# Decoder layer with attention, cross-attention and a gated FFN: other places in the rounds for score blocks, maxima, projections, splits and the gate step

## What is computed

```python
def _L0_attn_ref(x, Wq, Wk, Wv, Wo, gamma, beta):
    q = x @ Wq.T
    k = x @ Wk.T * scale
    v = x @ Wv.T
    ...
    qk = jnp.where(causal, qk, -jnp.inf)
    attn = jax.nn.softmax(qk, axis=-1)
    ...
    return ln @ Wo.T
...
x = x + _L0_attn_ref(_layernorm(x, axis=-1), ...)
x = x + _L0_xattn_ref(ctx_1024, ctx_1024, _layernorm(x, axis=-1), ...)
x = x + _L0_ffn_ref(_layernorm(x, axis=-1), ...)
...
    gates = entmax_bisect(logits)
    gates = jnp.where(gates > THRESH, gates, 0.0)
    h = jax.nn.relu(jnp.einsum('td,edf->etf', xt, W1) + b1[:, None, :])
    y = jnp.einsum('etf,efd->etd', h, W2) + b2[:, None, :]
    out = jnp.einsum('etd,te->td', y, gates)
```

## Time and profile before

| what | value |
|---|---|
| median of 3 runs | 665.8 us (664.77 to 667.24) |
| profiled execution | 664.33 us |
| its span, first to last instruction | 662.6 us |
| busy: PE, DVE, ACT, POOL | 93%, 70%, 62%, 55% |
| granted clock of PE, mean | 0.991 |
| length of rounds 0 to 6, from H 0 to the next H 0 | 72.85, 73.45, 73.59, 73.59, 73.60, 73.56, 66.63 us |
| round 7 and the end | 55.2 us |

### The profile page before, as it was taken

How to read it: one execution, slowest core, us unless ns; L and a number is a source line. 1 busy time by engine, 2 the same in 40 slices (tenths; PEclk the granted TensorE clock), 3 DMA queues, 4 the chain that set the end, 5 groups by cost and what they waited for, 6 DMA issues and landing times.

```text
span 662.6 us, 15729 instructions
## 1 busy us (share of the span) xinstructions
PE 618.6 (93%) x5263; PEld 459.8 (69%) x5263; DVE 464.3 (70%) x996; ACT 408.0 (62%) x780; POOL 363.9 (55%) x599
## 2 busy tenths in 40 slices
PE   5488879999999999999999999999999999998997
PEld 3355557777677767777678767777677767776775
DVE  4495984679747986689747986599557984656544
ACT  4239476755777566755766557755776567665543
POOL 8625565445663737444763746544753756464363
PEclk9889999999999999999999999999999999999999
DMA  6705100530027000630036000720045000700230
GB/s 187 230 17 169 45 4 18 127 117 4 19 45 208 10 8 14 151 107 2 18 67 191 0 20 0 162 95 2 18 98 159 2 2 6 159 2 1 55 88 16
DMA packets 39195, 43.76 MB, mean 66 GB/s; under 512 B 2922, under 2 KB 23670, under 8 KB 39158
## 3 DMA queue, kind: packets, MB, share of 16 engines
...
...
## 4 chain that ended last, share of the span: by engine, by line
PE 77%; DVE 8%; ACT 6%; POOL 3%; issue 2%; DMA 2%; SPq 2%; ACTq 0%; DVEq 0%; POOLq 0%
PE h_ps L1038 10%; PE y_ps L1038 9%; PE h_ps L1040 8%; PE h_ps L1039 8%; PE y_ps L1040 8%; PE y_ps L1039 8%; DVE negmax L1657 5%; PE sbuf_m L1149 5%; PE sbuf_s L1132 3%; PE sbuf_s L1104 2%; ACT prob L1462 2%; PE sbuf_s L1149 2%; PE sbuf_s L1053 1%; PE sbuf_s L1066 1%; PE sbuf_m L1038 1%
## 5 line engine op out<-in xcount | busy, mean ns | idle before, releaser
L1773 DVE SCALAR_TENSOR_TENSOR h_lo<-h_ps,h_hi 128x512 fp32r<-128x512 f32 x256 | 172.2, 682 | 120.3 <-ACT h_hi L1481 119.4
L1481 ACT ACTIVATE h_hi<-h_ps 128x512 fp32r<-128x512 f32 x256 | 152.1, 601 | 129.7 <-PE h_ps L1040 127.7
L1038 PE MATMUL h_ps<-fT_lo,w_hi 128*128 128x512 f32 x256 | 111.6, 436 | 4.1 <-DVE fT_lo L1626 2.7
L902 POOL TENSOR_SCALAR_AFFINE_SELECT prob<-prob 128x512 f32<-128x512 f32 x128 | 79.8, 642 | 60.7 <-ACT prob L1462 57.2
L1462 ACT ACTIVATE prob<-sbuf_s 128x768 f32<-128x768 f32 x124 | 95.2, 813 | 25.7 <-PE sbuf_s L1132 25.7
L1038 PE MATMUL y_ps<-h_lo,w_hi 128*128 128x512 f32 x255 | 106.9, 419 | 1.5 <-ACT y_sb L1490 1.5
L1657 DVE TENSOR_REDUCE negmax<-sbuf_s 128x4 f32<-128x1024 f32 (+1 forms) x91 | 106.9, 1212 | 0.1
L1039 PE MATMUL h_ps<-fT_hi,w_lo 128*128 128x512 f32 x256 | 101.2, 395 | 0.0
L1040 PE MATMUL h_ps<-fT_hi,w_hi 128*128 128x512 f32 x256 | 101.1, 395 | 0.0
L1040 PE MATMUL y_ps<-h_hi,w_hi 128*128 128x512 f32 x255 | 100.8, 395 | 0.0
L1039 PE MATMUL y_ps<-h_hi,w_lo 128*128 128x512 f32 x255 | 100.7, 395 | 0.0
...
## 6 DMA issues: line engine op xcount, KB each, us to landing
...
```

The source lines that it names most:

```text
L902: pool.affine_select(out=v, in_=v, compare_op=ALU.is_ge, fill=0.0, base=0, pattern=[[0, 2], [0, 2], [1, P]], channel_multiplier=-1).then_i ...
L1038: pe.matmul(out_ap, w_hi, m_lo, start=start, stop=False)
L1481: act.activation(h_hi[:, c % HB, :], h_ps[:, c % 2, :], ACT.Relu).then_inc(hhi_made, 1)
L1773: dve.scalar_tensor_tensor(out=h_lo[:, c % HB, :], in0=h_ps[:, c % 2, :], scalar=0.0, in1=h_hi[:, c % HB, :], op0=ALU.max, op1=ALU.subtrac ...
```

## The change

Numbers in the tables Z_STEPS, A_STEPS and X_STEPS are others; no function changes, no step is added or taken away, and the first phase and the last store are as before. All rounds are affected. A few of the lines of the diff, those that the text below speaks of:

```diff
-    Step("MAX", 6, "s", pe=26.02, dve=26.01),
-    Step("MAX", 7, "t", pe=26.03, dve=26.02),
-    Step("MT", 0, "m", pe=27.01, dve=26.03, sp=1.5),
+    Step("MAX", 6, "s", pe=26.02, dve=25.5134),
+    Step("MAX", 7, "t", pe=26.5255, dve=26.019),
+    Step("MT", 0, "m", pe=27.017, dve=26.5403, sp=1.5),
...
-    Step("MT", 1, "s", pe=32.51, dve=31.01, sp=1.75),
-    Step("SC", 2, "s", pe=33.51, act=33.51, pool=7.25),
-    Step("SC", 3, "t", pe=33.52, act=33.52, pool=7.5),
+    Step("MT", 1, "t", pe=32.5233, dve=31.5177, sp=1.75),
+    Step("SC", 2, "s", pe=33.5049, act=35.001, pool=7.25),
+    Step("SC", 3, "t", pe=40.5171, act=38.0238, pool=7.5),
...
-    Step("NA", 2, "-", act=31.01),
-    Step("T3", 0, "m", pe=32.52, act=31.02, dve=31.02),
+    Step("NA", 2, "-", act=30.503),
+    Step("T3", 0, "m", pe=32.51, act=32.5218, dve=33.5204),
...
-    Step("TH", 0, "-", pool=0),
+    Step("TH", 0, "-", pool=0.5),
...
-    Step("GV", 0, "-", dve=7.01),
+    Step("GV", 0, "-", dve=6.02),
...
-    Step("GT", 0, "m", pe=9.51, act=9.52, sp=0.25),
+    Step("GT", 0, "m", pe=10.0113, act=9.52, sp=0.25),
```

More of the change, by code:

```diff
@@ L78 @@
 Z_STEPS = [
[L79 to L86, removed]
+    Step("SZ", 0, "-", dve=8.5162, pool=2.75),
+    Step("NZ", 0, "-", act=12.5242),
+    Step("T1", 0, "t", pe=14.0063, act=14.0174, dve=14.0075),
@@ L87 @@
+    Step("Q", 0, "m", pe=16.0132, act=15.5254, dve=15.0077),
+    Step("K", 0, "s", pe=16.5178, act=16.0037, dve=16.0094, sp=1.25),
+    Step("V", 0, "t", pe=16.5269, dve=16.0165),
+    Step("MAX", 0, "s", pe=21.51, dve=21.0096),
+    Step("MAX", 1, "t", pe=22.5153, dve=21.5186),
     Step("MAX", 2, "s", pe=23.51, dve=23.01),
-    Step("MAX", 3, "t", pe=23.52, dve=23.02),
+    Step("MAX", 3, "t", pe=24.5197, dve=23.0227),
     Step("MAX", 4, "s", pe=25.01, dve=24.02),
-    Step("MAX", 5, "t", pe=25.02, dve=24.03),
@@ L101 @@
-    Step("SC", 2, "s", pe=33.51, act=33.51, pool=7.25),
-    Step("SC", 3, "t", pe=33.52, act=33.52, pool=7.5),
+    Step("MAX", 5, "t", pe=26.0193, dve=24.5335),
+    Step("MAX", 6, "s", pe=26.02, dve=25.5134),
+    Step("MAX", 7, "t", pe=26.5255, dve=26.019),
+    Step("MT", 0, "m", pe=27.017, dve=26.5403, sp=1.5),
+    Step("MAX", 8, "s", pe=28.5083, dve=28.0125),
+    Step("MAX", 9, "t", pe=29.0146, dve=28.0245),
+    Step("SC", 0, "s", pe=29.51, act=29.51, pool=6.5),
+    Step("SC", 1, "t", pe=30.0203, act=29.52, pool=6.75),
@@ L103 @@
+    Step("MAX", 10, "s", pe=30.51, dve=30.0102),
+    Step("MAX", 11, "t", pe=30.518, dve=30.5183),
+    Step("MT", 1, "t", pe=32.5233, dve=31.5177, sp=1.75),
+    Step("SC", 2, "s", pe=33.5049, act=35.001, pool=7.25),
+    Step("SC", 3, "t", pe=40.5171, act=38.0238, pool=7.5),
     Step("XL", 0, "-", sp=0),
@@ L106 @@
 A_STEPS = [
[L107 to L116, removed]
@@ L117 @@
-    Step("SC", 12, "s", pe=10.51, act=9.53, pool=2.75),
-    Step("SC", 13, "t", pe=10.52, act=9.54, pool=3.25),
+    Step("PV", 0, "m", pe=1.5203, act=4.5089),
+    Step("SC", 4, "s", pe=1.5379, act=1.5058, pool=0),
+    Step("SC", 5, "t", pe=2.0331, act=1.5198, pool=0.25),
+    Step("SC", 6, "s", pe=3.5086, act=3.5153, pool=0.75),
+    Step("SC", 7, "t", pe=4.0216, act=3.5266, pool=1),
+    Step("SC", 8, "s", pe=5.0086, act=5.0196, pool=1.5),
+    Step("SC", 9, "t", pe=6.0084, act=5.0246, pool=2),
@@ L119 @@
+    Step("PV", 1, "m", pe=6.0108, act=6.5048),
+    Step("SC", 10, "s", pe=6.0198, act=6.5219, pool=2.25),
+    Step("SC", 11, "t", pe=7.0198, act=7.5058, pool=2.5),
+    Step("SC", 12, "s", pe=10.51, act=9.53, pool=3),
+    Step("SC", 13, "t", pe=10.5146, act=9.5385, pool=3.25),
     Step("PV", 2, "m", pe=10.52, act=9.55),
     Step("SC", 14, "s", pe=11.02, act=10.01, pool=3.5),
-    Step("SC", 15, "t", pe=11.03, act=10.02, pool=3.75, sp=0.75),
-    Step("BT", 0, "s", pe=12.01, dve=10.02),
-    Step("BT", 1, "m", pe=12.02, dve=12.01),
+    Step("SC", 15, "t", pe=11.5314, act=10.0163, pool=3.75, sp=0.75),
@@ L124 @@
+    Step("BT", 0, "s", pe=12.01, dve=10.5201),
+    Step("BT", 1, "m", pe=12.02, dve=10.5206),
     Step("PV", 3, "t", pe=12.03, act=12.01),
-    Step("SA", 0, "-", dve=12.04, pool=4),
+    Step("SA", 0, "-", dve=12.039, pool=4),
     Step("BT", 2, "t", pe=12.51, dve=12.02),
[L127 to L137, removed]
-    Step("NA", 2, "-", act=31.01),
-    Step("T3", 0, "m", pe=32.52, act=31.02, dve=31.02),
+    Step("BT", 3, "m", pe=12.52, dve=12.03),
+    Step("NA", 0, "-", act=15.5127),
+    Step("TA", 0, "m", pe=18.0101, act=18.0075, dve=18.0084),
@@ new lines @@
+    Step("WO", 0, "s", pe=19.5132, dve=19.5116),
+    Step("SA", 1, "-", dve=20.5127, pool=5.25),
+    Step("NA", 1, "-", act=23.5086),
+    Step("T2", 0, "m", pe=24.5099, act=24.5121, dve=24.0109),
+    Step("XS", 0, "m", pe=26.0056, act=26.0103, dve=25.5068),
+    Step("PT", 0, "s", pe=27.0159, act=26.0109, dve=26.5217),
+    Step("SA", 2, "-", dve=28.0373, pool=6.25),
+    Step("XO", 0, "m", pe=28.5245, dve=28.0259),
+    Step("NA", 2, "-", act=30.503),
+    Step("T3", 0, "m", pe=32.51, act=32.5218, dve=33.5204),
@@ L143 @@
 X_STEPS = [
-    Step("TH", 0, "-", pool=0),
-    Step("LG", 0, "s", pe=1.01, dve=1.01),
+    Step("TH", 0, "-", pool=0.5),
+    Step("LG", 0, "s", pe=1.01, dve=1.5076),
     Step("TH", 1, "-", pool=1.25),
-    Step("TH", 2, "-", pool=1.5),
+    Step("TH", 2, "-", pool=1.75),
     Step("YM", 0, "-", pool=4.25),
     Step("YM", 1, "-", pool=4.5),
-    Step("YM", 2, "-", pool=5),
-    Step("YM", 3, "-", pool=5.25),
+    Step("YM", 2, "-", pool=4.75),
+    Step("YM", 3, "-", pool=5),
     Step("YM", 4, "-", pool=5.5),
@@ L154 @@
     Step("CP", 0, "-", pool=6),
-    Step("YM", 6, "-", pool=6.5),
-    Step("GV", 0, "-", dve=7.01),
+    Step("YM", 6, "-", pool=7),
+    Step("GV", 0, "-", dve=6.02),
     Step("YM", 7, "-", pool=7.75),
-    Step("GT", 0, "m", pe=9.51, act=9.52, sp=0.25),
+    Step("GT", 0, "m", pe=10.0113, act=9.52, sp=0.25),
 ]
```

## The result

The changed kernel takes 677.26 us (median of four runs, 675.96 to 678.37) against 665.79 for the kernel before, run beside it: a ratio of 1.017, 95% interval 1.014 to 1.02. It is slower by 1.7%, as forecast, and the time is 1.3 us over the 676.0 predicted. The profiled execution took 676.36 us (span 674.6) against 664.33 (662.6).

What follows compares the result with a forecast made beforehand. PE's issue order was taken to bound the kernel (PE busy 93% of the span). Losses of 9.0 + 0.7 + 1.6 = 11.3 us on 664.33 gave 675.6, or 677.1 from the median; forecast 676.0, range 668.5 to 680.0.

Steps and rivals of the forecast that it cites:

- The signs that I named: Trace signs: 1.2 us gap before H9, DVE idle over 1 us, mass at H0 + 15.8, excess 0.3 later, rounds 75.1.
- Place 1: GV ahead of l7 on DVE waits for POOL's gate chain, delaying H9: 1.04 + 0.25 us in rounds 0 to 6.
- The 0.25 for excess: After H0, SC4's mask on POOL runs beside L1722 on DVE and stretches it, so TH0 starts 0.25 us later.
- the 0.12 that I priced for it: By the shared-port rule POOL's first mask waits for L1718, TH0 some 0.12 us later; kept out of the sum.
- Place 2: Round border: MAX6 early makes drop_a, NA2, h31, l31 late, so next H0 is 0.26 us later, in six rounds.
- the terms of a tenth that it left out: Two opposite terms of about a tenth: later exps of SC2 and SC3, and H10 no longer behind GV.
- Most other moves pass under cover: Other reordered steps have inputs ready before their engine arrives and readers half a slot later or more, so cost nothing.
- block switches stay as many: On PE each small block keeps a neighbour of the same kind, so switches between block kinds do not change.
- The small loss: Rival: GV misses POOL's masks and takes 1.0 us, stall 0.3 before H9; about 669.5 us; chance 0.14.
- No difference: Rival: the mass comes a whole microsecond earlier, l7 is in time and the border stays; 665.8 us; chance 0.13.
- Faster: Rival: PE's three stops behind Y27 close, l31 ending by about 391.4; 1.1 us a round, about 659 us; chance 0.09.
- The larger loss: Rival: POOL resumes late behind the round's border, 0.7 us more a round; 681 us; chance 0.04.

Runs made afterwards that it cites:

- e2: Kernel before with only GV moved ahead of l7 on DVE; 675.06 us, ratio 1.0119, rounds 1 to 5 mean 74.62 us.
- e5: Changed kernel with GV, the seven border steps and GT put back; 666.95 us, ratio 0.9979 to the kernel before, rounds 73.29 us.
- e3: Changed kernel with the seven border steps put back, GV still ahead of l7; 676.45 us, ratio 1.0118 to the kernel before, rounds 74.34 us.
- e4: Changed kernel with GV and the seven border steps put back; 668.45 us, ratio 1.0015 to the kernel before, rounds 73.79 us.
- e1: Changed kernel with only GV put back behind l7 on DVE; 671.94 us, ratio 1.0057 to the kernel before, rounds 74.21 us.
- e8: Changed kernel with POOL's SZ moved right behind TH2, so no mask runs beside GV; 679.29 us in a single run, rounds 75.08 us.

## Why the prediction was right, and where not

**Direction and mechanism: right.** GV ahead of l7 is the loss: 1.06 us a round alone (e2), and 1.05 in the whole change as well (e5 to e3, 73.29 to 74.34, together with GT). The signs that I named are in the trace, some of them at another size: the gap before H9 put down to h_lo (a bracket of 0.76, for about 1.2), DVE idle for 1.99 between l6 and GV, the mass at H0 + 15.81, excess later (by 0.52, for 0.3; it is 0.32 in e3 and e4, and the rest is the 0.20 of l0 and l1), a wait that goes from before MT1 to before T3 and Y31, and rounds of 74.76, for about 75.1.

**Place 1, 1.29 a round: too high by a quarter of a microsecond.** Measured are 1.05. The 0.25 for excess have a real cause: L1722 beside SC4's mask took 0.74 instead of 0.43, in the changed kernel and in e4 alike, and TH0 starts 0.32 later in e4 than before. Here is e4:

```profile
328.06 0.43 DVE L1718 TENSOR_TENSOR over<-below 128x256 f32<-128x256 f32 x1
328.52 0.74 DVE L1722 SCALAR_TENSOR_TENSOR over<-over 128x256 f32<-128x256 f32 x1
```

```profile
328.34 1.42 POOL L902 TENSOR_SCALAR_AFFINE_SELECT prob<-prob 128x512 f32<-128x512 f32 x2 [0.36 <-ACT prob L1462]
329.91 0.30 POOL L934 TENSOR_SCALAR moments<-excess 128x32 f32<-128x32 f32 x1 [0.15 <-DVE excess L1725]
```

With that, the working has H9 at H0 + 18.56, and it stands at 18.32. The 0.24 are three pieces: the mass came at 15.81 and not 15.62 + 0.25 = 15.87; GV follows it by 0.08 and not by 0.2; and l7 starts 1.69 behind GV's start and not 1.74. The 18.32 hold the 0.13 of the late SC4, which belong to the border; in e3, which is without them, the mass comes at 15.71 and H9 at 18.22, so against that the working is 0.34 too late, and half of it is the mass. Its sums also slip by 0.02 to 0.03 on the way (326.68 is carried on as 326.66; 330.14 + 2.95 + 0.81 is 333.90 and not 333.87), which changes nothing.

The rule of the Trainium skill, "SBUF — State Buffer", section "Who interferes with whom", that a two-input DVE instruction and a GpSimd instruction reading SBUF exclude each other, would have made POOL's first mask wait for L1718. In e4 the first mask starts at 328.34, while L1718 runs until 328.49, and the 0.12 that I priced for it are not there: TH0 is 0.32 late, the 0.34 of the sum without the rule. That DVE is held up is seen; that POOL is, at most in the second mask of the pair (1.42 for two, where four took 2.41).

**Place 2, 0.26 a round: too low.** 0.42 (after to e3, e4 to e1). I had the chain (MAX6 late, drop_a late, NA2, h31, l31, MT1, T3), and it makes 0.27 in e1 as priced. But I counted only what shows at the border; the other 0.15 are the late SC4 in the next round, which the working put among the terms of a tenth that it left out (the later exps of SC2 and SC3). One line of the working does not add up as it stands: 392.47 and 0.08 + 0.76 + 0.69 are 394.00, and 393.84 comes out with the 0.08 taken off. The trace has it the second way: MT1 is drawn as starting 0.08 ahead of l31's end, and from l31's end to T3's on DVE it is 1.36, for 1.37.

**"Most other moves pass under cover": wrong, they gain 0.27 a round.** I wrote that PE stands still only behind Y27. It also waited for l8 at H10, 0.13 a round, where the timeline names no gap. And I wrote that block switches stay as many; between Q and WO the moves give back 0.14, for a reason that stays open. GT's move behind H10 is not in the working at all (its term of a tenth at H10 was GV's); it costs 0.4 to 0.5 by itself, though it seems to cost nothing beside GV's new place.

**The sum.** Rounds 0 and 6 lose more at H9 than the five between them (it stands 1.16 later in round 0 and 1.67 in round 6, and GV is 2.3 long in both); round 7 loses the 0.7 that I worked out (0.69). Place 1: 1.16 + 5 × 1.05 + 1.67 + 0.69 = 8.8, for 9.7. Border: 6 × 0.42 = 2.5, for 1.6. The others: about 6 × −0.27 = −1.6, for 0. Together 9.7, for 11.3, and the rounds grew by 9.8; how round 0 divides among the three is taken from the other rounds, not measured. That the profiled time was still 676.36, over the 675.6 of the sum, is the 2.2 us ahead of round 0. So three terms were off by about 0.9, 0.9 and 1.6 us, these 2.2 were not foreseen, and that the total came within 1.3 us is luck; the direction and the largest term are not.

**The rivals.** The small loss (GV unstretched) is what e8 shows, for its H9 alone; in the changed kernel the masks do meet GV, as in the forecast. No difference is out: the mass was no earlier. Faster is out at the place that I gave: l31 ended at H0 + 73.2 and not by 71.4. The larger loss (POOL late behind the border) does not show: POOL stands idle for 0.30 ahead of SC4's mask, waiting for ACT's exp, and drop_a comes late from DVE, not from POOL.
